# One GNN kernel on one core: the gate, statistics, norm and dense stage ahead of the third pass as a pipeline over pairs of blocks

## The chip, the cores and the metric

One NeuronCore of a Trainium2 chip. Its engines are TensorE (PE; its weight loads stand apart as PEld), VectorE (DVE), ScalarE (ACT), GpSimd (POOL) and SyncE (SP, which here only issues DMAs). The metric is the device time of one execution in microseconds; less is better.

## The reference

`x` has 6250 rows of 256 floats, and there are 106250 edges. Four layers follow one another, each as `x = layernorm(x + L(x))`. The stage in question lies between layer 1 and the first edge loop of layer 2:

```python
# end of layer 1: gate is one row of 256, spa one number a node
L1 = x * spa + x + x * gate
x = _layernorm(x + L1)                          # (v - mean) / sqrt(var + 1e-5)
# layer 2, ahead of its sum over the edges
h = jnp.concatenate([x[row], x[col]], axis=-1)
msgs = silu(h @ W1.T + b1) @ W2.T + b2
```

The product with `W1.T` is made once a node and not once an edge: `x @ A + b1` and `x @ B` are two tables of 256 columns. The edge loop takes a row of the first by a product with a one-hot matrix, and a row of the second (`q_table`) by a gather from DRAM.

## The kernel before, in words

The rows of `x` stand in SBUF as 50 blocks of 128 rows (`x_sb`, NBE = 50), in the tile `big`; two blocks are a pair, and there are 25 (PAIRS). Every engine has its own program; they meet only at semaphores, and each engine's wait holds whatever follows it in that program. The stage between the layers runs as these steps, one after the other:

- **Gate and statistics** (VectorE, L1887): for each pair, (gate + 2 + spa) times x in place (L1891), then mean and variance of each row (L1768, L1772), copied aside (L1774). Each step waits for the one ahead of it (`link`).
- **Norm**: one square root and one reciprocal for all blocks (`normalizers`, L1785 to L1792), then 50 times `normalize` in place (L1798).
- **Store**: once all 50 blocks are done, SyncE writes all of `x_sb` to `x2_table` in DRAM in one DMA (L399) and waits for it. From here on `x_sb` isn't read again before the third pass is over; its place is taken by `p3`.
- **Clear** (VectorE): the accumulator `acc` is set to zero (L1900).
- **Dense**: SyncE loads the blocks of a pair back from `x2_table` to `staged_x` (L406); TensorE turns a block (4 of them a pair, L757); ScalarE copies it to `turned` (L1140); TensorE multiplies by the two halves of W1.T (L931 for q, L933 and the bias L934 for the other), in fp32; ScalarE copies q to `hq` (L1151), which SyncE stores to `q_table` (L411); VectorE splits the other product into three bf16 parts with four instructions (L1908 to L1911) and writes them to `p3`. TensorE turns pair i and multiplies pair i-1 in one turn of its loop.
- **Third pass** (888 tiles of 128 edges): GpSimd gathers rows of `q_table` (L531), and waits ahead of the first for all of its stores; VectorE tells TensorE that it may start by `pass_ready`.

GpSimd has nothing to do in this stage. `x_sb` is 256 floats a block, `p3` is three times 256 bf16 numbers, that is 384 floats a block, in the same tile `big`.

## Time and profile before

| | us |
|---|---|
| median of 3 runs | 7678.52 |
| lowest, highest | 7677.68, 7684.38 |
| the profiled execution, device time | 7685.36 |
| its span | 7683.8 |
| busy in it: PE, DVE, POOL, ACT | 5491.4, 4781.7, 4367.7, 1817.7 |

Times in the rows are microseconds from the start of the span, and the duration of one instruction is in ns where the row says mean. An `x4` is four instructions taken together. What stands in brackets is the idle time of that engine ahead of the instruction and what ended it; SPq is the queue of SyncE. PEclk is TensorE's granted clock: 1.00 is 2.4 GHz and 0.50 is 1.2 GHz. A `MATMUL` on fp32 data shows as two instructions.

### The profile page before, as it was taken

How to read it: one execution, taken by the hardware profiler on the slowest of the kernel's cores; microseconds unless marked ns; L12 is line 12 of the kernel's file. 1: busy time of each engine (PE TensorE's matmuls, PEld its weight loads, DVE VectorE, ACT ScalarE, POOL GpSimd, SP SyncE). 2: the span in 40 equal slices, each digit the busy share in tenths (PEclk: the TensorE clock that was granted, in tenths of full speed). 3: DMA queues.
4: the chain of work that ended last, by engine and by line, in shares of the span. 5: the costliest groups of instructions: out<-in, count | busy, mean ns of one | idle time of the engine just before them, and what ended most of it. 6: DMA issues, size and time to landing. Idle time of an engine off the chain costs nothing.

```text
span 7683.8 us, 131635 instructions
## 1 busy us (share of the span) xinstructions
PE 5491.4 (71%) x23656; PEld 3592.6 (47%) x23657; DVE 4781.7 (62%) x13613; ACT 1817.7 (24%) x3090; POOL 4367.7 (57%) x4491
## 2 busy tenths in 40 slices
PE   5566667799999979399999979815655555656650
PEld 4333334467777658265555545413333333333330
DVE  8878787567777769667777755564344433444435
ACT  4100000168888720033333323300000000000000
POOL 0377777557777730027777730005777777777760
PEclk7577778799999985599999989966555555555555
DMA  3244444443333313233333350011111123111122
GB/s 91 47 124 124 123 125 130 105 133 103 103 103 103 104 26 120 70 100 105 104 105 105 105 92 0 6 45 56 52 52 52 52 51 52 52 52 52 52 51 65
DMA packets 317649, 612.93 MB, mean 80 GB/s; under 512 B 90563, under 2 KB 177804, under 8 KB 317130
## 3 DMA queue, kind: packets, MB, share of 16 engines
q0 software_dynamic: 185408, 469.86, 23.1%
q1 hardware_dynamic: 132106, 141.78, 6.1%
q14 instruction: 113, 0.93, 0.0%
q8 instruction: 22, 0.36, 0.0%
HBM read 573.87 MB, written 43.84 MB: 80 GB/s over the span
## 4 chain that ended last, share of the span: by engine, by line
PE 47%; issue 19%; DVE 15%; DMA 12%; DVEq 3%; POOL 3%; ACT 0%; SPq 0%; POOLq 0%; ACTq 0%
PE bank L751 14%; PE bank L835 8%; PE bank L824 6%; DMA ring<-q_table,stage_i 5%; PE bank L784 5%; DMA ring<-fwd_table,stage_i 3%; DMA ring<-bwd_table,stage_i 2%; POOL ring L531 2%; DVE oh L1652 2%; PE bank L727 2%; DVE ring L1946 1%; DVE big L1503 1%; PE bank L719 1%; PE bank L985 1%; PE bank L986 1%
## 5 line engine op out<-in xcount | busy, mean ns | idle before, releaser
L1641 DVE TENSOR_TENSOR acc<-bank,acc 128x256 f32 (+1 forms) x3552 | 1272.2, 358 | 1681.5 <-PE bank L751 1324.8
L751 PE MATMUL bank<-ring,oh 128*128 128x128 f32 x3552 | 1336.1, 485 | 916.1 <-issue 619.3
L751 PEld LDWEIGHTS bank<-ring,oh 128*128 128x128 f32 x3552 | 884.7, 312 | 1367.6 <-issue 1026.9
L531 POOL DMA_INDIRECT ring<-fwd_table,stage_i x888 | 846.5, 953 | 1006.1 <-issue 937.3
L531 POOL DMA_INDIRECT ring<-q_table,stage_i x888 | 843.3, 950 | 900.9 <-issue 795.1
L531 POOL DMA_INDIRECT ring<-h_table,stage_i x888 | 860.2, 969 | 374.8 <-PE bank L824 192.9
L531 POOL DMA_INDIRECT ring<-bwd_table,stage_i x888 | 842.2, 948 | 274.9 <-issue 156.3
L1166 ACT ACTIVATE ring<-big 128x889 f16<-128x889 f16 x840 | 874.1, 1041 | 199.6 <-PE bank L835 164.5
L835 PE MATMUL bank<-ring,big 128*128 128x445 f16 (+1 forms) x3360 | 773.8, 352 | 0.0
L1652 DVE TENSOR_SCALAR oh<-iota,d_loc,d_norm 128x128 f32<-128x128 f32 x1776 | 658.6, 374 | 70.3 <-DVE big L1725 20.3
L557 POOL DMA_INDIRECT big<-x_and_degree,stage_i x536 | 552.2, 1030 | 201.9 <-issue 118.6
L824 PE MATMUL bank<-ring,oh 128*128 128x256 f32 x1776 | 574.1, 407 | 53.5 <-DVE oh L1652 47.4
L784 PE MATMUL bank<-big,oh 128*128 128x256 f32 x1072 | 443.6, 548 | 228.4 <-DVE oh L1652 224.3
L835 PEld LDWEIGHTS bank<-ring,big 128*128 128x128 f16 x3360 | 483.6, 144 | 161.6 <-issue 0.3
L970 PE MATMUL bank<-ring,oh 128*128 128x257 f32 x1776 | 533.6, 415 | 8.1 <-ACT ring L1251 3.9
L954 PE MATMUL bank<-big,oht 128*128 x2664 | 412.6, 282 | 91.1 <-DVE ring L1946 43.8
L1937 DVE TENSOR_TENSOR acc<-bank,acc 128x257 f32 x888 | 377.1, 425 | 148.6 <-DVE acc L1937 50.7
L784 PEld LDWEIGHTS bank<-big,oh 128*128 128x128 f32 x1072 | 234.2, 255 | 408.7 <-DVE oh L1652 290.2
L557 POOL DMA_INDIRECT ring<-x_and_degree,stage_i x352 | 359.6, 1022 | 107.1 <-issue 69.8
L1946 DVE TENSOR_TENSOR ring<-bank,ring 128x512 f32<-128x512 f32 x444 | 305.0, 687 | 157.8 <-DMA ring<-q_table,stage_i 142.0
L1251 ACT ACTIVATE ring<-ring 128x512 f32<-128x512 f32 x444 | 280.1, 631 | 481.3 <-DVE ring L1946 481.1
L824 PEld LDWEIGHTS bank<-ring,oh 128*128 128x128 f32 x1776 | 298.8, 194 | 198.4 <-issue 76.4
(385 smaller groups left out, 7023.3 us busy)
## 6 DMA issues: line engine op xcount, KB each, us to landing
big<-places_in_block SPq DMA_DIRECT2D x111, 256.0 KB, 3.5
acc<-places_in_block SPq DMA_DIRECT2D x74, 384.0 KB, 3.5
ring<-h_table,stage_i POOLq DMA_INDIRECT x888
ring<-q_table,stage_i POOLq DMA_INDIRECT x888
ring<-fwd_table,stage_i POOLq DMA_INDIRECT x888
ring<-bwd_table,stage_i POOLq DMA_INDIRECT x888
big<-x_and_degree,stage_i POOLq DMA_INDIRECT x536, 3.0
h_table<-hq SPq DMA_DIRECT2D x50, 128.0 KB, 1.7
```

Source lines behind the costliest of these rows:

```text
L531: pool.indirect_dma_start(out=gbuf[:, u % RING, 0:width], out_offset=None, in_=table, in_offset=bass.IndirectOffsetOnAxis(ap=stage_i[:, v, ...
L557: pool.indirect_dma_start(out=first_bufs[v][:, r, 0:D + 1], out_offset=None, in_=xd_dram, in_offset=bass.IndirectOffsetOnAxis(ap=stage_i[: ...
L751: pe.matmul(bank[u % 4][:, 0:width], oh[:, u % 4, :], gbuf[:, u % RING, 0:width], start=True, stop=True).then_inc(S["mm"], 1)
L784: pe.matmul(bank[u % 4][:, 0:D], oh[:, u % 4, :], first_bufs[v][:, r, 0:D], start=True, stop=True).then_inc(S["mm"], 1)
L824: pe.matmul(bank[u % 4][:, 0:D], oh[:, u % 4, :], gbuf[:, r, 0:D], start=True, stop=True).then_inc(S["mm"], 1)
L835: mm = pe.matmul(bank[4 + 2 * k + h][:, 0:hi - lo], low_k[2 * w + k][:, :, r:r + 1].rearrange("p n a -> p (n a)"), high_k[(u + 2 * RING) % ...
L954: mm = pe.matmul(bank[2 + u // 2][:, u % 2 * D:(u % 2 + 1) * D], oht[:, h % 2, u * P:(u + 1) * P], p3[:, s, ds(b, 1), :].rearrange("p a f ...
L970: pe.matmul(bank[4 + u][:, 0:D + 1], oh[:, t % 12, :], msg[:, t % RING, :], start=True, stop=True).then_inc(S["l2_c"], 1)
L1166: act.activation(high_k[u % 3], iota_h, ACT.Sign, bias=high_bias[:, ds(j, 1)]).then_inc(S["sort_high"], 1)
L1641: dve.tensor_tensor(to, bank[u % 4][:, 0:width], to, ALU.add).then_inc(S["accd"], 1)
L1652: o = dve.tensor_scalar(oh[:, u % 4, :], iota[:, :], loc[:, t], weight[:, t], ALU.is_equal, ALU.mult)
L1946: dve.tensor_tensor(msg[:, both, 0:D], bank[2 + t // 2 % 2][:, :].rearrange("p (r f) -> p r f", r=2), gbuf[:, both, 0:D], ALU.add).then_in ...
```

## The change

The stage is written as a pipeline over the 25 pairs. Every engine runs turns t = 0, 1, 2, ...; in turn t it does its step for pair t - lag, where the lag is the step's own. The turns short of the largest lag and those at the end are written out, the others are a loop of two turns (`staggered`). The lags:

| step | engine | pair in turn t |
|---|---|---|
| gate; statistics; their sum to mean and variance | DVE | t; t-1; t-2 |
| square root | ACT | t-3 |
| reciprocal, norm into `x2_buf` | DVE | t-4 |
| store of `x2_buf` to `x2_table` | SP | in the order x2(0), x2(1), q(0), x2(2), q(1), ... |
| turning (4) | PE | t-5 |
| copy to `turned` | ACT | t-6 |
| the two products | PE | t-7 |
| first part of p3, copy to `hq` | ACT | t-8 |
| first rest | DVE | t-9 |
| second part of p3 | ACT | t-10 |
| third part of p3 | DVE | t-11 |

Blocks are taken from the last to the first (`countdown`), and `p3` is laid out by block, so that its parts can be written to `big` while lower blocks of `x_sb` are still to be read. The normed pair goes to one of two buffers `x2_buf`, in the upper half of `ring`; TensorE turns it from there, so that nothing is loaded back. SyncE stores it pair by pair. GpSimd sets `acc` to zero, from `spa_in` on. The counter `p_diff` starts at 2, `x2_out` at 0 and `d_h` at NBE + 2.

The change, cut to its core:

```diff
+def staggered(engine, turns, lag, step):
+    for t in range(lag):
+        step(t, t % 2)
+    twice = (turns - lag) // 2
+    with engine.Fori(0, twice) as i:
+        for k in range(2):
+            step(i * 2 + lag + k, (lag + k) % 2)
+    for t in range(lag + 2 * twice, turns + lag):
+        step(t, t % 2)
...
-        p3 = big[:, :].bitcast(BF16).rearrange("p (s b f) -> p s b f", s=3, f=D)
+        p3 = big[:, :].bitcast(BF16).rearrange("p (b s f) -> p s b f", s=3, f=D)
...
+        x2_buf, rest_p = ([ring[:, LATER + a + 512 * k:LATER + a + 512 * (k + 1)] for k in range(2)] for a in (0, 1024))
...
-            sp.wait_ge(S["x2_done"], NBE)
-            sp.dma_start(x2_dram.rearrange("(b p) f -> p b f", p=P), x_sb).then_inc(S["p_loaded"], 16)
-            sp.wait_ge(S["p_loaded"], 16)
...
+            def store_x2(i, k, n):
+                sp.wait_ge(S["x2_done"], i + 1)
+                apart(sp, S["sp_waited"])
+                if not (isinstance(i, int) and i == 0):
+                    sp.wait_ge(S["x2_out"], i * 16)
+                apart(sp, S["sp_waited"])
+                sp.dma_start(x2_dram[ds(n * P, 2 * P), :].rearrange("(q p) f -> p q f", p=P),
+                             x2_buf[k].rearrange("p (q f) -> p q f", q=2)).then_inc(S["x2_out"], 16)
+            def store_q(i, n):
                 for q in range(2):
-                    sp.wait_ge(S["d_t"], i * 2 + q + 1 + 2 * NBE)
-                    sp.dma_start(staged_x[:, q, :], dense_rows(x2_dram, i * 2 + q)).then_inc(pair["p_in"][q], 16)
-            def store_q(i):
-                for q in range(2):
-                    sp.wait_ge(S["d_h"], i * 2 + q + 3 + NBE)
-                    sp.dma_start(dense_rows(q_dram, i * 2 + q), hq[:, q, :]).then_inc(pair["tab_out"][q], 16)
-            load_pair(0)
-            load_pair(1)
-            with sp.Fori(2, PAIRS) as i:
-                load_pair(i)
-                store_q(i - 2)
-            store_q(PAIRS - 2)
-            store_q(PAIRS - 1)
+                    sp.wait_ge(S["d_h"], i * 2 + 4 + NBE)
+                    apart(sp, S["sp_waited"])
+                    sp.dma_start(dense_rows(q_dram, n + q), hq[:, q, :]).then_inc(pair["tab_out"][q], 16)
+            store_x2(0, 0, 2 * (PAIRS - 1))
+            with sp.Fori(0, PAIRS // 2) as i:
+                for k in range(2):
+                    n = countdown(sp, i * 2 + 1 + k, PAIRS)
+                    store_x2(i * 2 + 1 + k, 1 - k, n)
+                    store_q(i * 2 + k, n + 2)
+            store_q(PAIRS - 1, 0)
+            sp.wait_ge(S["x2_out"], 16 * PAIRS)
...
+            pool.wait_ge(S["spa_in"], 1)
+            pool.memset(acc_flat, 0.0).then_inc(S["acc_clear"], 1)
...
+            def d4_turn(t, par):
+                i, k2 = t - 5, (par + 1) % 2
+                if in_range(i, PAIRS):
+                    pe.wait_ge(S["x2_done"], i + 1)
+                    pe.wait_ge(S["d_at"], i * 2 + 2 * NBE)
                     for q in range(2):
+                        for k in range(2):
+                            mm = pe.transpose(bank[4 + k2][:, k * D + q * P:k * D + (q + 1) * P],
+                                              x2_buf[k2][:, q * D + k * P:q * D + (k + 1) * P], ident[:, :])
+                    mm.then_inc(S["d_t"], 2)
+                i, k2 = t - 7, (par + 1) % 2
+                if in_range(i, PAIRS):
+                    pe.wait_ge(S["d_at"], i * 2 + 4 + 2 * NBE)
+                    pe.wait_ge(S["p_diff"], i + 1)
+                    pe.wait_ge(S["d_h"], i * 2 + NBE)
+                    for q in range(2):
+                        for k in range(2):
+                            pe.matmul(bank[6 + k2][:, q * D:(q + 1) * D], turned[:, k2, k * D + q * P:k * D + (q + 1) * P], w_ab[:, k, 0:D], start=(k == 0), stop=False)
+                        pe.matmul(bank[6 + k2][:, q * D:(q + 1) * D], ones_b[:, :], bias_parts[:, D:2 * D], start=False, stop=True)
+                    for q in range(2):
+                        for k in range(2):
+                            mm = pe.matmul(bank[2 + k2][:, q * D:(q + 1) * D], turned[:, k2, k * D + q * P:k * D + (q + 1) * P], w_ab[:, k, D:2 * D], start=(k == 0), stop=(k == 1))
+                    mm.then_inc(S["d_m"], 2)
+            staggered(pe, PAIRS, 7, d4_turn)
...
+            def d4_functions(t, par):
+                last = countdown(act, t, PAIRS)
+                i, k2 = t - 3, (par + 1) % 2
+                if in_range(i, PAIRS):
+                    act.wait_ge(S["x2_agg"], i + 1)
+                    act.activation(std_k[k2].rearrange("p q a -> p (q a)"), mv_k[k2][:, :, 1:2].rearrange("p q a -> p (q a)"), ACT.Sqrt,
+                                   bias=cols[:, 10:11]).then_inc(S["x2_std"], 1)
+                i, k2 = t - 6, par
+                if in_range(i, PAIRS):
+                    act.wait_ge(S["d_t"], i * 2 + 4 + 2 * NBE)
+                    act.wait_ge(S["d_m"], i * 2 + 2 * NBE)
+                    act.activation(turned[:, k2, :], bank[4 + k2][:, :], ACT.Copy).then_inc(S["d_at"], 2)
+                i, k2 = t - 8, par
+                if in_range(i, PAIRS):
+                    n = last + 16
+                    act.wait_ge(S["d_m"], i * 2 + 4 + 2 * NBE)
+                    act.activation(p3[:, 0, ds(n, 2), :], bank[6 + k2][:, :].rearrange("p (q f) -> p q f", q=2), ACT.Copy).then_inc(S["p_high"], 1)
+                    if not (isinstance(i, int) and i == 0):
+                        for q in range(2):
+                            act.wait_ge(pair["tab_out"][q], BASE["tab_out"] + i * 16)
+                    act.activation(hq[:, :, :], bank[2 + k2][:, :].rearrange("p (q f) -> p q f", q=2), ACT.Copy).then_inc(S["d_h"], 2)
+                i, k2 = t - 10, par
+                if in_range(i, PAIRS):
+                    n = last + 20
+                    act.wait_ge(S["p_diff"], i + 1 + 2)
+                    act.activation(p3[:, 1, ds(n, 2), :], rest_p[k2].rearrange("p (q f) -> p q f", q=2), ACT.Copy).then_inc(S["p_mid"], 1)
+            act.activation(cols[:, 12:13], half_less[:, 0:1], ACT.Sqrt)
+            staggered(act, PAIRS, 10, d4_functions)
...
+            def d4_turn(t, par):
+                last = countdown(dve, t, PAIRS)
+                both_of = lambda s, n: p3[:, s, ds(n, 2), :]
+                by_block = lambda a: a.rearrange("p (q f) -> p q f", q=2)
+                i = t - 4
+                if in_range(i, PAIRS):
+                    dve.wait_ge(S["x2_std"], i + 1)
+                    inverse = std_k[par].rearrange("p q a -> p (q a)")
+                    dve.reciprocal(inverse, inverse).then_inc(S["x2_inv"], 1)
+                i = t - 11
+                if in_range(i, PAIRS):
+                    dve.wait_ge(S["p_mid"], i + 1)
+                    dve.tensor_tensor(both_of(2, last + 22), by_block(rest_p[1 - par]), both_of(1, last + 22), ALU.subtract).then_inc(S["p_split"], 1)
+                i = t - 4
+                if in_range(i, PAIRS):
+                    dve.wait_ge(S["x2_inv"], i + 1)
+                    dve.wait_ge(S["d_t"], i * 2 + 2 * NBE)
+                    if not (isinstance(i, int) and i < 2):
+                        dve.wait_ge(S["x2_out"], i * 16 - 16)
+                    for q in range(2):
+                        n = last + 8 + q
+                        o = dve.tensor_scalar(x2_buf[par][:, q * D:(q + 1) * D], x_of(n), mv_k[par][:, q, 0:1], std_k[par][:, q, :], ALU.subtract, ALU.mult)
+                    o.then_inc(S["x2_done"], 1)
+                i = t - 9
+                if in_range(i, PAIRS):
+                    dve.wait_ge(S["p_high"], i + 1)
+                    if not (isinstance(i, int) and i < 2):
+                        dve.wait_ge(S["p_split"], i - 1)
+                    dve.tensor_tensor(by_block(rest_p[1 - par]), by_block(bank[7 - par][:, :]), both_of(0, last + 18), ALU.subtract).then_inc(S["p_diff"], 1)
+                i = t
+                if in_range(i, PAIRS):
+                    for q in range(2):
+                        n = last + q
+                        o = dve.scalar_tensor_tensor(x_of(n), gate_bc[:, :], sm["spa"][:, ds(n, 1)], x_of(n), ALU.add, ALU.mult)
+                    o.then_inc(S["x2_mul"], 1)
+                i = t - 2
+                if in_range(i, PAIRS):
+                    dve.wait_ge(S["x2_stat"], i + 1)
+                    if not (isinstance(i, int) and i < 2):
+                        dve.wait_ge(S["x2_done"], i - 1)
+                    apart(dve, S["waited"])
+                    for q in range(2):
+                        o = dve.bn_aggr(mv_k[par][:, q, :], stats_k[par][:, q, :])
+                    o.then_inc(S["x2_agg"], 1)
+                i = t - 1
+                if in_range(i, PAIRS):
+                    dve.wait_ge(S["x2_mul"], i + 1)
+                    if not (isinstance(i, int) and i < 2):
+                        dve.wait_ge(S["x2_agg"], i - 1)
+                    for q in range(2):
+                        n = last + 2 + q
+                        o = dve.bn_stats(stats_k[(par + 1) % 2][:, q, :], x_of(n))
+                    o.then_inc(S["x2_stat"], 1)
+            staggered(dve, PAIRS, 11, d4_turn)
+            dve.wait_ge(S["p_split"], PAIRS)
+            dve.wait_ge(S["acc_clear"], 2)
+            dve.wait_ge(S["x2_out"], 16 * PAIRS)
```

## Rows read from the trace of the kernel before

**Rows 1.** Instructions in order of time: the marks between the steps of the stage.

```profile
3126.15 0.88 DVE L1891 SCALAR_TENSOR_TENSOR big<-gate_bc,spa,big 128x256 f32 x2 [0.46 <-DVE gate_bc L1883]
...
3228.07 0.40 SPq L399 DMA_DIRECT2D x_table<-big  x1
3248.40 6.86 SPq L406 DMA_DIRECT2D staged_x<-x_table  x6
3251.12 10.77 DVE L1900 MEMSET acc<- 128x12850 f32 x1 [23.07 <-issue]
```

**Rows 2.** The chain that ended last, in order of time, at the end of the stage.

```profile
3383.16 1.70 DMA q_table<-hq
```

**Rows 3.** The dense step as one stretch: its length, then the columns of the first line.

```profile
core 0: us, PE busy (x) PEld busy (x) DVE busy (x) ACT busy (x) POOL busy (x), PEclk, DMA share, GB/s
3262.00:3385.00 123.00, 116.19 (x520) 81.69 (x520) 78.46 (x201) 31.09 (x94) 0.00 (x0) 1.00 0.30 99
```

**Rows 4.** Instructions in order of time: one pair of the dense step.

```profile
3264.16 0.73 PEld L931 LDWEIGHTS bank<-wbuf,turned 128*128 128x128 f32 x4 [2.51 <-DVE big L1911]
3266.68 0.38 ACT L1151 ACTIVATE hq<-bank 128x256 f32<-128x256 f32 x1
3267.23 2.50 SPq L411 DMA_DIRECT2D q_table<-hq  x2
3268.43 0.98 PE L757 MATMUL bank<-ident,staged_x 128*128 128x128 f32 x4
3268.53 0.38 ACT L1140 ACTIVATE turned<-bank 128x256 f32<-128x256 f32 x1 [1.48 <-PE bank L934]
3269.15 0.73 PEld L931 LDWEIGHTS bank<-wbuf,turned 128*128 128x128 f32 x4
3270.27 0.98 SPq L406 DMA_DIRECT2D staged_x<-x_table  x2
```

**Rows 5.** Groups of instructions by line: busy us, mean ns of one, idle before.

```profile
L1798 DVE TENSOR_SCALAR big<-big,mean,rstd x50 | 20.6, 412 | 4.7 <-DVE rstd L1785 0.4
L1768 DVE BATCH_NORM_STATS2 stats<-big 128x6 f32 x50 | 18.8, 418 | 3.8 <-DVE big L1891 3.8
L1946 DVE TENSOR_TENSOR ring<-bank,ring 128x512 f32<-128x512 f32 x444 | 305.0, 687 | 157.8 <-DMA ring<-q_table,stage_i 142.0
L1246 ACT ACTIVATE oht<-bank 128x512 bf16<-128x512 f32 x79 | 47.2, 597 | 80.5 <-PE bank L962 80.5
```

**Rows 6.** The issues of line L411: ns min/median/max, first and last start.

```profile
L411 SPq DMA_DIRECT2D q_table<-hq x50: 332/356/362, 3259.4 to 3383.2; - x50
```

**Rows 7.** DMA issues: KB each, median us from issue to landing.

```profile
x_table<-big SPq DMA_DIRECT2D x1, 6400.0 KB, 20.3
q_table<-hq SPq DMA_DIRECT2D x50, 128.0 KB, 1.7
```

**Rows 8.** Two pauses of TensorE, in the brackets, in order of time.

```profile
3386.05 0.45 PE L962 MATMUL bank<-ident,oh 128*128 128x128 f32 x1 [3.33 <-issue]
...
4517.86 0.46 PE L970 MATMUL bank<-ring,oh 128*128 128x257 f32 x1 [3.92 <-ACT ring L1251]
```

**Rows 9.** Stretches around changes of the granted clock (columns as in Rows 3).

```profile
3259.00:3260.00 1.00, 1.00 (x6) 0.90 (x5) 1.00 (x1) 0.22 (x1) 0.00 (x0) 0.97 0.00 0
3386.00:3388.00 2.00, 1.09 (x4) 0.72 (x4) 0.73 (x4) 0.60 (x1) 1.70 (x2) 0.50 0.14 31
3392.00:3393.00 1.00, 0.52 (x5) 0.39 (x5) 0.27 (x1) 0.98 (x2) 0.70 (x2) 0.91 0.26 82
4516.00:4518.00 2.00, 0.14 (x1) 0.17 (x2) 1.19 (x3) 0.73 (x2) 0.00 (x0) 1.00 0.00 0
```

**Rows 10.** TensorE's first products of the stage, in order of time.

```profile
3254.32 1.40 PEld L931 LDWEIGHTS bank<-wbuf,turned 128*128 128x128 f32 x4
3258.39 1.04 PEld L931 LDWEIGHTS bank<-wbuf,turned 128*128 128x128 f32 x4 [0.22 <-issue]
```

**Rows 11.** Who SyncE's queue waited for in this stage: us in total, times, longest.

```profile
SPq L411 <- ACT hq L1151: 65.0, 50, 3.9
```

More of the change, by code:

```diff
@@ L42, in runs, with countdown, in_range @@
     return g >= lag if first else g < lag if last else True
+def staggered(engine, turns, lag, step):
[7 more added lines that the diff above has]
+        step(t, t % 2)
+def countdown(engine, t, pairs):
+    return (pairs - 1 - t) * 2 if isinstance(t, int) else engine.snap(t * -2 + (pairs - 1) * 2, min_val=0, max_val=2 * (pairs - 1))
+def in_range(t, turns):
+    return not isinstance(t, int) or 0 <= t < turns
 class Chain:
@@ L1324, in _ @@
             dve.sem_inc(S["slot_prod"], 3)
-            for n in ("d_res", "p_split", "g_ag2", "g_xn", "f_res", "f_out"):
+            for n in ("d_res", "p_diff", "g_ag2", "g_xn", "f_res", "f_out"):
                 dve.sem_inc(S[n], 2)
@@ L1432, in place_blocks @@
                 link(dve.tensor_copy(blk[:, 512:TC], bank[first + 1][:, 0:TC - 512]))
+            dve.memset(cols[:, 10:11], 1e-5)
             link(dve.memset(cols[:, 8:9], 1e-12))
@@ L1885, in _ @@
             dve.wait_ge(S["spa_out"], 1)
-            with dve.Fori(0, PAIRS) as i:
-                chain.enter(i, 4)
-                for q in range(2):
-                    n = i * 2 + q
-                    o = dve.scalar_tensor_tensor(x_of(n), gate_bc[:, :], sm["spa"][:, ds(n, 1)], x_of(n), ALU.add, ALU.mult)
-                link(o)
-                pair_statistics(i)
-            chain.leave(PAIRS)
-            normalizers()
-            with dve.Fori(0, NBE) as b:
-                normalize(x_of(b), b).then_inc(S["x2_done"], 1)
@@ L1912, in _ @@
-            chain.leave(PAIRS)
-            dve.wait_ge(S["p_split"], NBE + 2)
+            def d4_turn(t, par):
[51 more added lines that the diff above has]
+                    o.then_inc(S["x2_stat"], 1)
```

45 lines of the change are left out of this document (7 added, 38 removed).

## The prediction

> **What bounds the kernel now.** I read the page first (span and engines), then the instructions in order of time from the gate to the first gather of the third pass, then stretches, groups and waits of that part. Nothing outside it is touched. The stage runs from 3126.15, the first gate [rows 1], to 3384.86, when the last store of q lands [rows 2]: 258.7 us of 7685.36. The reader is to see three parts that follow one another. Gate, statistics and norm take VectorE alone 101.9 us (3126.15 to 3228.07). The store of all x2 and its wait take 20.3 more, during which nothing computes (3228.07 to 3248.40), and the clearing of the accumulator another 10.8 until 3261.9, over which only three groups of products are made [rows 1]. From 3262 on TensorE is the bound: 116.2 of 123 us busy at a granted clock of 1.00, that is 2.4 GHz [rows 3], one pair from 3264.16 to 3269.15, 4.99 us [rows 4]. VectorE has 78.5 us of work in these 123 and ScalarE 31.1 [rows 3].
>
> **The change, part by part.**
>
> Work per pair after it. VectorE: gate 0.88 [rows 1], statistics 2 x 0.418, norm 2 x 0.412, two subtractions of 512 columns at 0.687 each (the row of a subtraction or sum of that size with one operand in PSUM) [rows 5], some 0.4 for the means and the reciprocal: 4.3 us, and about 5 with the gaps between them. TensorE: the same ten products, 4.4 us from their first weights to ScalarE's start (3264.16 to 3268.53), and four turnings of 0.98 together [rows 4]: 5.3. ScalarE: four copies at 0.597 [rows 5] and a root. SyncE: three issues in place of four. So by work alone a turn is about 5.3 us, and by that the change would gain about 100 us (the first rival). The reload of x2 goes, and so do the 10.8 us of clearing: GpSimd has no other work until the q stores land, so it lies beside them; if it held VectorE up for all its length, that is at most the 10.8 us that VectorE's own clearing took [rows 1]. I take 0. The other layout of p3 and the order from the last block down leave every instruction's size as it is: 0.
>
> What is on the path is a circle of waits that the change makes itself. SyncE's order is x2(m+1), q(m), x2(m+2), q(m+1). A store of q waits for ScalarE's copy of q, and in SyncE's program the next store of x2 stands behind it. VectorE's norm of pair i waits until x2(i-2) has landed (it has two buffers), so it also waits for q(i-4). The lags don't help, because the product that makes q(i-4) itself waits for VectorE: the products of pair j wait for `p_diff` of j+1, which starts at 2, so for the first rest of pair j-2, and VectorE's program has that one right behind the norm of j+3. Followed round: norm of i; first rest of i-5; products of i-3; the two copies of i-3; q(i-3); x2(i-1); its landing; norm of i+1. One round is one pair, and none of its steps lies beside another. Its length:
>
> - norm 0.82 and first rest 0.69 [rows 5]: 1.5
> - products: 4.4 at full clock [rows 4]
> - ScalarE, first part and then q, 2 x 0.597 [rows 5]: 1.2
> - SyncE: 0.17 from the end of a copy (3267.06) to the issue of its store [rows 4]; 0.62 from one issue to the next (0.98 less the 0.36 of an issue [rows 6]); then 0.62 to 0.90 to the store of x2, as 0.90 is what lies between the second q issue (3269.37) and the next load (3270.27) [rows 4]. I take 0.75: 1.5 in all
> - landing of 256 KB: 128 KB took 1.7, and 6400 KB 20.3 [rows 7], so 1.7 + 128 x 18.6 / 6272 = 2.1
> - three hand-overs between engines and the address arithmetic behind each wait, 0.1 each: 0.3. No row shows these waits alone; ends 0 and 1
>
> Sum 11.0 us. TensorE works 4.4 + 1.0 of it and then waits 5.6. That brings in the clock. In the trace TensorE paused for 3.33 us at the end of the stage [rows 8] and came back at 0.50, 1.2 GHz, where it stayed until about 3392.1 [rows 9], 6.1 us later. But after a pause of 3.92 us [rows 8] at 4517.86 the clock was still 1.00 [rows 9]. A pause of 5.6 is longer than both, so I take it that the clock falls in every round. At 1.2 GHz one block's products took 4.07 (3254.32 to 3258.39) [rows 10] against 2.2 (half of the pair's), so a pair takes 8.1 if the clock never rises. It rises during them: 4.7 us after the first products (3254.32 to 3259.0) [rows 9, 10] and 6.1 in the other case. With 4.7 slow the pair takes 4.7 + (8.1 - 4.7) / 2 = 6.4, with 6.1 it takes 7.1. I take 6.4, since here nothing interrupts the burst, and get a round of 13.0; the ends are 11.0 and 14.8.
>
> The Trainium skill, page "TensorE: Matmul & The Clock Gate", section "HAM oscillation — how this bites in real kernels", tells of a kernel whose products come in bursts with a wait for data between them, and whose clock fell anew in each wait. By that rule the round of 11.0 doesn't occur; by the row with the pause of 3.92 us it could.
>
> Sum. Start: pair 0 is normed after four short turns, 4 x 0.88 + 3 x 0.84 + 0.4 + 1.0 and gaps, 7.8 us; pair 2 after two more turns of 3.2, at 14.2; then four turnings and the products of pair 0 at low clock, to 22.0; its copies 23.3; SyncE and landing 3.6, so the norm of pair 4 starts at 26.9. The products of pair 1 need no first rest and follow at once, so the norm of pair 5 starts at 32.2. From there 19 rounds to the norm of pair 24: 19 x 13.0 = 247. End: norm and first rest 1.6, products 6.4, turnings 1.0, three pairs of products without a pause 3 x 4.3, copies 1.2, last store 0.17 + 0.62 + 1.7: 25.6. Together 304.8 us in place of 258.7, **46 us more**. Of what went away, 101.9 of gate and norm now lie beside the rounds, 20.3 + 10.8 are gone; late instead is the store of x2 behind the store of q. The profiled execution would take 7731; it lies 6.9 above the median of the runs, so **7725** there.
>
> **The rivals.**
>
> 1. *The engines run free* (faster): if SyncE's order does not hold the norm back, a turn is bound by TensorE's 5.3 us, 25 x 5.3 = 133, with 8 ahead and 4 behind and a slow start of 4, about 149; if by VectorE's 5 to 5.5 with 11 turns of fill and drain, about 165. 157 gives 102 less: 7577. For it: SyncE waited 65.0 us in all for ScalarE's q in this stage before and delayed nobody [rows 11]. Against it: there the loads behind were two pairs ahead; here the norm needs what is behind, within the same round. It holds if the store of x2 can be two pairs earlier than the waits say. A sentence of the Trainium skill points this way: "DMA: Bandwidth & Descriptors", section "Issuing engines are not separate DMA queues", has it that spreading DMAs over engines saves only the time to initiate them. By it SyncE's order would cost 1.5 us a turn, which is hidden; it doesn't speak of a DMA that stands behind another's wait.
> 2. *The circle holds, the clock stays* (no change): 32.2 + 19 x 11.0 + 23.6 = 264.8, 6 more: 7685. For it the pause of 3.92 us, against it that of 3.33 [rows 8, 9].
> 3. *The circle holds and the clock never rises*: 32.2 + 19 x 14.8 + 27.3 = 340.7, 82 more: 7761. For it that the burst of 6 to 8 us is hardly longer than the 4.7 to 6.1 after which it rose [rows 9, 10].
>
> The turning point between slower and faster is a round of about 10.7 us.
>
> **Chances and range.** The forecast (a round of 12 to 14.2, 7705 to 7748) 0.60; clock stays 0.14; clock never rises 0.11; engines run free 0.12; something else 0.03. 0.2% or 15 us is what a measurement can tell. Faster by more: the free engines and a little of the rest, 0.14. Within: most of the second rival, 0.12. Slower: 0.74. The range takes in the second rival and the third, 7680 to 7765, and leaves out the first, whose place is 100 us off.
>
> **What would show it.** A stage of some 305 us between first gate and first gather; a gate instruction every 13 us from turn 9 on where it is now every 3; VectorE's longest waits ahead of the norm, ended by the DMA to x2_table; SyncE waiting for ScalarE's q; TensorE's clock falling and rising every round with pauses of 5 to 6 us. With free engines the norm would come every 5.3 us and the store of x2 would be issued right after it. A pause without a fall of the clock gives rival 2. If the norm waits for ScalarE or TensorE and not for a DMA, the circle is another one than mine.

## The result, and the profile after

The kernel after the change takes 7766.15 us (median of 5 runs, 7735.88 to 7774.06), beside 7681.53 us of the kernel before on the same chip (5 runs, 7677.68 to 7685.06): ratio 1.0103, 95% interval 1.0089 to 1.0117. It is slower by 85 us, where 46 were forecast. The range, 7680 to 7765, stood against 7678.52 for the kernel before, so it ended 86.5 above that kernel; the 84.6 measured are just inside it, beyond the 7705 to 7748 of the forecast itself, and next to the place of the third rival (82 more). The profiled execution is the one of 7766.15, its span 7764.3.

First the marks of the stage, as in [rows 1]: instructions in order of time, of the kernel after. Columns: start, us, engine, line, operation.

```profile
3130.52 1.67 DVE L1997 SCALAR_TENSOR_TENSOR big<-gate_bc,spa,big 128x256 f32<-128x256 f32 x4 [0.17 <-DVE gate_bc L1956]
...
3158.28 0.74 DVE L1984 TENSOR_SCALAR ring<-big,pair_small 128x256 f32<-128x256 f32 x2 [8.21 <-DMA x_table<-ring]
...
3165.97 0.73 DVE L1984 TENSOR_SCALAR ring<-big,pair_small 128x256 f32<-128x256 f32 x2 [5.30 <-DMA x_table<-ring]
...
3451.09 0.73 DVE L1984 TENSOR_SCALAR ring<-big,pair_small 128x256 f32<-128x256 f32 x2 [11.41 <-DMA x_table<-ring]
...
3469.93 4.33 SPq L440 DMA_DIRECT2D q_table<-hq  x3
```

The L1984 lines are the norms of pairs 4, 5 and 24. The last store of q is issued at 3473.9 (3469.93 + 4.33 less an issue of 0.33) and lands 1.7 us later, at 3475.6. So the stage is 345.1 us where it was 258.7 [rows 1, 2], 86.4 more, which accounts for the 84.6 between the kernels. Its three parts: 35.45 us to the norm of pair 5, 285.12 for the 19 rounds from there to the norm of pair 24 (15.01 each), and 24.5 for the end.

Second, one round of the circle, in order of time, of the kernel after.

```profile
3300.48 0.38 SPq L433 DMA_DIRECT2D x_table<-ring  x1
3302.77 0.74 DVE L1984 TENSOR_SCALAR ring<-big,pair_small 128x256 f32 x2 [11.20 <-DMA x_table<-ring]
3303.42 0.69 DVE L1992 TENSOR_TENSOR ring<-bank,big 128x512 f32<-128x512 f32 x1
...
3304.34 2.07 PE L968 MATMUL bank<-wbuf,turned 128*128 128x256 f32 x4 [6.78 <-DVE ring L1992]
...
3312.87 0.60 ACT L1290 ACTIVATE turned<-bank 128x512 f32<-128x512 f32 x1 [7.49 <-PE bank L972]
3313.37 0.59 ACT L1296 ACTIVATE big<-bank 128x512 f32 x1
3313.85 0.60 ACT L1300 ACTIVATE hq<-bank 128x512 f32<-128x512 f32 x1
3314.32 0.64 ACT L1306 ACTIVATE big<-ring 128x512 f32 x1
3314.70 0.93 SPq L440 DMA_DIRECT2D q_table<-hq  x2
3316.40 0.38 SPq L433 DMA_DIRECT2D x_table<-ring  x1
```

Every link of the predicted circle is there, each behind the one before: the store of x2, its landing and the norm 2.29 us later, norm and first rest (L1992) 1.34, hand-over 0.23, the products until ScalarE's first copy 8.53, ScalarE 1.58 to the end of the copy to `hq` (3314.45), 0.25 to its store, and 1.70 to the next store of x2. That is 15.92 us; rounds of this kind alternate with shorter ones. The brackets name the releasers: VectorE sat 11.20 us until the DMA to x2_table had landed, TensorE 6.78 until the first rest, ScalarE 7.49 until the products.

Third, the same as sums: who waited for whom between 3180 and 3440 (us in total, times, longest).

```profile
DVE ring L1984 <- DMA x_table<-ring: 210.3, 18, 12.4
PEld bank L968 <- issue: 129.4, 35, 7.1
ACT turned L1290 <- PE bank L972: 117.9, 17, 7.5
PE bank L968 <- DVE ring L1992: 101.1, 15, 6.9
```

SyncE's own waits in the whole stage (L27 lies in the helper `apart`, which is called right behind the wait):

```profile
SPq L27 <- ACT hq L1300: 275.1, 25, 13.5
```

Fourth, stretches (columns as in [rows 3]): the body of the stage, and single microseconds of three bursts of products, which start at 3304.34, 3320.16 and 3412.29.

```profile
3180.00:3430.00 250.00, 140.58 (x363) 91.13 (x364) 58.46 (x181) 38.47 (x81) 0.00 (x0) 0.63 0.10 34
...
3313.00:3314.00 1.00, 0.53 (x3) 0.23 (x2) 0.00 (x0) 1.00 (x3) 0.00 (x0) 0.85 0.00 0
...
3320.00:3321.00 1.00, 0.84 (x2) 0.76 (x3) 1.00 (x6) 0.00 (x0) 0.00 (x0) 0.50 0.00 0
3326.00:3327.00 1.00, 1.00 (x4) 0.82 (x3) 0.00 (x0) 0.00 (x0) 0.00 (x0) 0.53 0.00 0
3327.00:3328.00 1.00, 1.00 (x7) 0.85 (x7) 0.00 (x0) 0.06 (x1) 0.00 (x0) 1.00 0.00 0
...
3414.00:3415.00 1.00, 1.00 (x3) 0.52 (x3) 0.00 (x0) 0.00 (x0) 0.00 (x0) 0.50 0.00 0
3415.00:3416.00 1.00, 1.00 (x4) 0.66 (x3) 0.00 (x0) 0.00 (x0) 0.00 (x0) 0.65 0.00 0
3416.00:3417.00 1.00, 1.00 (x6) 0.66 (x5) 0.00 (x0) 0.00 (x0) 0.00 (x0) 1.00 0.00 0
```

TensorE is busy for 140.58 of 250 us and its mean granted clock is 0.63, where it was 116.19 of 123 at 1.00 [rows 3]. In the first burst the clock rises only at 3313.3, 9.0 us after the start and behind the products (ScalarE began to copy at 3312.87); in the second it rises 6.8 us after the start, in the third after 3.4. Over the 19 rounds the products take 8.5 and 7.4 to 7.8 us in turn, and 6.2 to 6.6 in the last few.

Last, something that the prediction had put at nothing. The first norm instructions of the stage and the clearing of `acc` by GpSimd, in order of time, of the kernel after:

```profile
3129.89 10.81 POOL L632 MEMSET acc<- 128x12850 f32 x1 [360.16 <-DVEq L1954]
...
3136.10 5.06 DVE L1984 TENSOR_SCALAR ring<-big,pair_small 128x256 f32<-128x256 f32 x2
...
3142.84 0.73 DVE L1984 TENSOR_SCALAR ring<-big,pair_small 128x256 f32<-128x256 f32 x2
```

The two instructions of pair 0 took 5.06 us, those of pair 1 0.73, and they ended 0.46 us behind the clearing (3136.10 + 5.06 = 3141.16 against 3129.89 + 10.81 = 3140.70), which is about one instruction of this kind: the first of the two was held until the clearing ended.

### The profile page after: what moved, and what is told of

It reads as the page before. It is cut to its first block, busy times and chain, and to the rows that moved or that the text cites. A ratio compares the mean times of both kernels' runs of the same rounds, so it can differ in the third digit from the quotient of the medians.

```text
span 7764.3 us, 130770 instructions
## 1 busy us (share of the span) xinstructions
PE 5559.9 (72%) x23656; PEld 3638.3 (47%) x23657; DVE 4718.5 (61%) x13460; ACT 1844.3 (24%) x3115; POOL 4373.5 (56%) x4492
## 4 chain that ended last, share of the span: by engine, by line
PE 24%; issue 13%; DMA 13%; DVE 5%; POOL 2%; DVEq 1%; SPq 0%; POOLq 0%; ACT 0%; ACTq 0%
PE bank L783 14%; DMA ring<-q_table,stage_i 6%; DMA ring<-fwd_table,stage_i 3%; DMA ring<-bwd_table,stage_i 2%; POOL ring L561 2%; DVE ring L2056 2%; PE bank L1024 1%; PE bank L1025 1%; PE bank L968 1%; PE bank L972 1%; PE bank L1009 1%; DVE oh L1723 1%; PE bank L1029 1%; PE bank L1032 1%; PE bank L993 1%
## 5 line engine op out<-in xcount | busy, mean ns | idle before, releaser
L783 PEld LDWEIGHTS bank<-ring,oh 128*128 128x128 f32 x3552 | 884.6, 311 | 1360.1 <-issue 977.9
L993 PEld LDWEIGHTS bank<-big,oht 128*128 128x128 bf16 x2664 | 255.6, 96 | 292.6 <-issue 209.3
```

What stands on the lines that cost most here:

```text
L783: pe.matmul(bank[u % 4][:, 0:width], oh[:, u % 4, :], gbuf[:, u % RING, 0:width], start=True, stop=True).then_inc(S["mm"], 1)
L993: mm = pe.matmul(bank[2 + u // 2][:, u % 2 * D:(u % 2 + 1) * D], oht[:, h % 2, u * P:(u + 1) * P], p3[:, s, ds(b, 1), :].rearrange("p a f ...
```

## The experiments

### The circle opened at SyncE: x2 stored two pairs ahead

Only the order of SyncE's stores changes; every wait keeps its value. In the kernel after, the store of x2 of pair m stands behind the q of pair m-2; here it stands behind that of pair m-4, and the first four wait for nothing of the circle.

```diff
-            store_x2(0, 0, 2 * (PAIRS - 1))
-            with sp.Fori(0, PAIRS // 2) as i:
-                for k in range(2):
-                    n = countdown(sp, i * 2 + 1 + k, PAIRS)
-                    store_x2(i * 2 + 1 + k, 1 - k, n)
-                    store_q(i * 2 + k, n + 2)
-            store_q(PAIRS - 1, 0)
+            for i in range(3):
+                store_x2(i, i % 2, 2 * (PAIRS - 1 - i))
+            with sp.Fori(0, (PAIRS - 3) // 2) as i:
+                for k in range(2):
+                    n = countdown(sp, i * 2 + 3 + k, PAIRS)
+                    store_x2(i * 2 + 3 + k, 1 - k, n)
+                    store_q(i * 2 + k, n + 6)
+            for m in range(PAIRS - 3, PAIRS):
+                store_q(m, 2 * (PAIRS - 1 - m))
```

> The changed kernel with one edit: SyncE issues the stores of x2 for pairs 0 to 2 first and then x2(m+3), q(m), so no store of x2 stands behind a store of q that isn't ready. Theory A (the circle norm, first rest, products, copies, store of q, store of x2, landing, norm sets the round of about 15.3 us that the changed kernel's profile shows): the circle is cut, the norm no longer waits for a landing, and a round falls to TensorE's 5.3 us at a clock of 1.00 (it then pauses under 1 us); the stage takes about 150 to 165 us in place of 345, and the kernel about 7580. Rival B (the lags themselves are too short, so that VectorE and TensorE wait for each other whatever SyncE does): the round stays over 10 us and the kernel over 7680. Rival C (the store to DRAM is what is slow, not its place): the norm still waits for the landing, round of 8 or more.

Measured: 7564.11 us (4 runs, 7562.13 to 7565.93), ratio to the kernel before 0.9848, interval 0.9831 to 0.9864. From its profile a stretch, a wait, and two stores of x2 that are one pair apart:

```profile
3150.00:3250.00 100.00, 100.00 (x470) 73.38 (x470) 67.67 (x207) 46.28 (x101) 0.00 (x0) 1.00 0.32 109
```

```profile
DVE ring L1986 <- DMA x_table<-ring: 2.1, 1, 2.1
```

```profile
3234.75 0.38 SPq L433 DMA_DIRECT2D x_table<-ring  x1
...
3239.19 0.38 SPq L433 DMA_DIRECT2D x_table<-ring  x1
```

TensorE is busy for all of the 100 us at full clock, VectorE waits 2.1 us for a DMA in that stretch, and a pair takes 4.70 us on average (the stores come 4.44 and 4.98 us apart in turn). The stage is 137.3 us, from 3129.20 to 3266.54. So the same instructions on every engine, with the same waits and one other order of issue, move the kernel by 202 us. The place of the store in SyncE's program is the cause, and this version beats both kernels.

### The same with one pair ahead

The store of x2 of pair m stands behind the q of pair m-3; the rest is as above.

```diff
+            for i in range(2):
+                store_x2(i, i % 2, 2 * (PAIRS - 1 - i))
+            with sp.Fori(0, (PAIRS - 3) // 2) as i:
+                for k in range(2):
+                    n = countdown(sp, i * 2 + 2 + k, PAIRS)
+                    store_x2(i * 2 + 2 + k, k, n)
+                    store_q(i * 2 + k, n + 4)
+            store_x2(PAIRS - 1, (PAIRS - 1) % 2, 0)
...
```

> The changed kernel with the store of x2 one pair earlier on SyncE than in the change: x2(m+2), q(m). Theory A says how long a round is: the same circle now goes round in two pairs, so at full clock its 11.7 us give 5.9 a pair, against 4.70 in x2_two_ahead, where TensorE was the bound; 19 pairs of 1.2 us make some 20 to 25 us, so the kernel at 7585 to 7595 if the clock stays at 1.00, and up to 7620 if it falls at times. If only the fact counts that a store of x2 stands behind one of q, as it still does here for the pair before, the kernel stays over 7700.

Measured: 7591.10 us (2 runs, 7587.71 to 7594.49), ratio 0.9879 (0.9859 to 0.9899). The waits of VectorE between 3180 and 3270:

```profile
DVE ring L1987 <- DMA x_table<-ring: 26.7, 13, 3.0
```

The granted clock over these 90 us is 0.91. The circle still closes, but with the other order one trip round it leads from the norm of pair i to that of i+2, so it serves two pairs: 12.0 us for two at a clock of 1.00 (from norm to norm, 3195.57 to 3207.60), and 13.6 from there on (3207.60 to 3221.22), where the clock falls once in every two pairs; the free engines need 9.4. A stage of 171.3 us lies between 345.1 and 137.3.

By the same count a trip serves three pairs when x2 is stored two pairs ahead. An estimate from the 12.0 us is then 4.0 a pair, less than the 4.70 for which TensorE is busy. So in that version the circle isn't gone: it is short enough to hold nobody up.

### The stores of q issued by ScalarE

SyncE stores x2 alone; ScalarE issues the store of q behind its own copy to `hq`.

```diff
-                    store_q(i * 2 + k, n + 2)
-            store_q(PAIRS - 1, 0)
...
                     act.activation(hq[:, :, :], ...).then_inc(S["d_h"], 2)
+                    act.wait_ge(S["d_h"], i * 2 + 4 + NBE)
+                    for q in range(2):
+                        apart(act, S["act_waited"])
+                        act.dma_start(dense_rows(q_dram, n + q), hq[:, q, :]).then_inc(pair["tab_out"][q], 16)
```

> The changed kernel with the stores of q issued by ScalarE, right after its copy, in place of SyncE; SyncE has only the stores of x2 left. Theory A: as with the other order on SyncE, a round of 5.3 to 5.6 us and the kernel at about 7580, as ScalarE has some 2.9 us of work a turn and the two issues and the wait for its own copy add about 1.5. Rival F (a queue of its own only saves the time to issue, 1.5 us a round): round of 13.5 to 14, kernel about 7725.

Measured: 7577.81 us (2 runs, 7576.57 to 7579.05), ratio 0.9865 (0.9845 to 0.9884). All stores of x2 in one row, in order of time:

```profile
3142.01 117.90 SPq L433 DMA_DIRECT2D x_table<-ring  x25
```

25 stores in 117.9 us are one in 4.9 us, and between 3150 and 3250 VectorE never waited for a DMA. It is 14 us behind the version with x2 two pairs ahead: ScalarE now issues too (between 3150 and 3250 its copy L1307 waited 14 times for issue, 19.1 us). This takes the link between the two stores out of SyncE's program altogether. The Trainium skill, page "DMA: Bandwidth & Descriptors", section "Issuing engines are not separate DMA queues", has it that spreading DMAs over engines saves only the time to initiate them. Here the spreading was worth 188 us (7766.15 against 7577.81, each beside about 7681 of before), since what it took away was a wait in the program of the issuing engine; the page doesn't speak of that case, and the measurement decides it.

### VectorE takes the first rest ahead of the norm

The first rest of pair t-9 moves ahead of the norm of pair t-4 within a turn of VectorE, so that the products of t-7 no longer stand behind the norm of t-4.

```diff
+                i = t - 9
+                if in_range(i, PAIRS):
+                    dve.wait_ge(S["p_high"], i + 1)
+                    ...
+                    dve.tensor_tensor(by_block(rest_p[1 - par]), by_block(bank[7 - par][:, :]), both_of(0, last + 18), ALU.subtract).then_inc(S["p_diff"], 1)
                 i = t - 4
                 if in_range(i, PAIRS):
                     dve.wait_ge(S["x2_inv"], i + 1)
...
-                i = t - 9
-                ...
```

> The changed kernel with SyncE's order kept and one edit in VectorE's turn: the first rest of pair t-9 ahead of the norm of pair t-4 and not behind it. Theory A: the circle then goes round only once in two pairs (norm of i-1, rest of i-5 comes ahead of norm of i, products of i-3, copies, store of q, store of x2, norm of i+1), so the round about halves: 7.7 to 9 us with the remaining waits, the stage about 195 to 245, the kernel about 7620 to 7660. Rival E (SyncE waiting for q is the whole cause, and VectorE's order is of no account): round and time as in the changed kernel, 7735 to 7775.

Measured: 7638.43 us (2 runs, 7638.34 and 7638.52), ratio 0.9944 (0.9924 to 0.9964). The waits between 3180 and 3300, and the stretch itself:

```profile
DVE ring L1991 <- DMA x_table<-ring: 63.1, 14, 5.7
```

```profile
3180.00:3300.00 120.00, 91.39 (x313) 59.80 (x313) 51.30 (x154) 32.91 (x70) 0.00 (x0) 0.81 0.19 64
```

A round (norm to norm) takes 7.8 us and 8.0 to 9.6 in turn, 8.4 on average, and the stage 214.1. VectorE still waits for the DMA, 4.5 us each time in place of 11.7 (210.3 / 18). So the link from norm to first rest in VectorE's program is part of the circle too; what remains is a shorter circle, not free engines.

### What the clock takes: TensorE kept busy in its pause

The circle stays, and TensorE gets products whose result nobody reads (128x512, fp32, from `ident` and `wbuf` into a bank that is free then) ahead of its wait for the first rest; they are work added, and nothing is left out. Five of them first, seven in a later kernel.

```diff
                 i, k2 = t - 7, (par + 1) % 2
                 if in_range(i, PAIRS):
+                    for f in range(5):
+                        pe.matmul(bank[0][:, :], ident[:, :], wbuf[:, 0:512], start=True, stop=True)
```

> The changed kernel with SyncE's order kept. TensorE makes five more fp32 products of 128x512 a turn, into a bank that nobody reads, ahead of its wait for the first rest; they only fill its pause. At full clock they take 5 x 0.85 = 4.3 us of a pause of 6.7. Theory A1 (the circle stays, and TensorE's low clock makes the products 8 us in place of 4.4): the clock stays near 1.00 in the stage, products take 4.4, a round falls from 15.3 to about 11.5 and the stage from 345 to about 275, the kernel to about 7700, and its runs spread less. Rival D (the products are slow for another reason, for instance their order or the waits between them): they stay at 8 us, the round grows by what the extra work sticks out of the pause, and the kernel is at 7770 or above.

Measured: 7760.36 us (4 runs, 7759.62 to 7761.28), ratio 1.0102 (1.0085 to 1.0119). This missed, and the rows say why. TensorE in order of time, and the microsecond in which the clock fell:

```profile
3288.25 4.46 PE L964 MATMUL bank<-wbuf,ident 128*128 128x512 f32 x10
3295.19 1.13 PE L970 MATMUL bank<-wbuf,turned 128*128 128x256 f32 x4 [2.49 <-DVE ring L1994]
```

```profile
3296.00:3297.00 1.00, 1.00 (x4) 0.53 (x3) 1.00 (x4) 0.23 (x1) 0.00 (x0) 0.62 0.00 0
```

The five filled 4.46 of some 7 us. A pause of 2.49 us stayed, and the clock fell just behind it, within the products. Of 18 such pauses between 3197 and 3436 (2.3 to 2.7 us) the clock fell at or just behind 12 and stayed up at 6. The rounds took 13.7 us on average in place of 15.01, and the ends of the stage grew. So this run couldn't price the clock, and the filler was lengthened to seven.

> As fill_pause, with seven products of 128x512 in place of five: at full clock 7 x 0.89 = 6.2 us of a pause of 6.7 (in fill_pause the trace showed a pause of 2.5 us left, and the clock fell 3.7 us after it began). Theory A1 (the circle stays, the pause puts the clock down and so makes the products 8 us): with a pause of 0.5 us the clock stays at 1.00, the products take 4.4, a round 11.8 and the stage about 280 us in place of 345; the kernel at 7700 to 7715. Rival D (the products are slow for another reason than the clock): round of 15 or more, kernel at 7765 or above.

Measured: 7733.74 us (4 runs, 7731.35 to 7734.88), ratio 1.0064 (1.0047 to 1.0081). The stretch, VectorE's wait in it, and TensorE in order of time:

```profile
3180.00:3400.00 220.00, 204.86 (x673) 112.61 (x673) 60.45 (x186) 44.74 (x93) 0.00 (x0) 1.00 0.13 45
```

```profile
DVE ring L1986 <- DMA x_table<-ring: 151.3, 18, 9.7
```

```profile
3300.31 6.17 PE L964 MATMUL bank<-wbuf,ident 128*128 128x512 f32 x14
3307.26 1.13 PE L970 MATMUL bank<-wbuf,turned 128*128 128x256 f32 x4 [0.78 <-DVE ring L1994]
```

The clock is now 1.00 over 220 us, TensorE is busy for 204.86 of them, and the kernel is still 49 us slower than before. By the parts of the stage some 27 of these are the filler's own, at its two ends (below); the other 22 are the circle's, without any low clock in its rounds. The round is 11.8 us where the second rival's sum said 11.0, and 15.01 without filler. So the clock was worth 3.2 us a round, 61 us over 19 rounds; only 32 of them show in the time, and it missed the 7700 to 7715 expected. The filler of 6.2 us a turn also stands ahead of products at the two ends of the stage, where there was no pause to fill, and start and end together are 86.8 us (46.2 and 40.6 of a stage of 311.1) in place of 60.0. A busy TensorE at full clock isn't a bound: with 93% busy this stage was 311.1 us, and with less work on TensorE it was 137.3.

The kernel after was run once more beside fill_all and x2_one_ahead.

> The changed kernel as it is, beside the others on this chip. Its five runs so far gave 7736 to 7774. Theory A1: no round's wait changes, only in how many rounds the clock comes up early; expected 7735 to 7775 again, and more spread than the kernels whose clock stays up.

Measured: 7769.97 us (4 runs, 7742.11 to 7776.52), ratio 1.0104 (1.0082 to 1.0126), as the first time. Its runs spread over 34 us, and over 38 the first time, where those of the two kernels with filler spread over 1.7 and 3.5. In its profile the 19 rounds take 288.6 us, in the first one 285.1: the last three rounds were 13.2 to 13.7 us long there, here one was.

### GpSimd's clearing and VectorE's norm

The kernel before with one part of the change alone: GpSimd clears `acc`, VectorE no longer does.

```diff
-            link(dve.memset(acc_flat, 0.0))
...
+            pool.wait_ge(S["spa_in"], 1)
+            pool.memset(acc_flat, 0.0).then_inc(S["acc_clear"], 1)
...
+            dve.wait_ge(S["acc_clear"], 2)
```

> The kernel before with one part of the change alone: GpSimd clears acc from spa_in on, VectorE doesn't. Expected: VectorE's 10.8 us go, but TensorE worked beside them until 3260.9; it gains the 2.5 us that its products of pair 1 waited for VectorE, and perhaps a few more where its clock rises no earlier: 2 to 8 us, so 7673 to 7679, hardly measurable. If the clearing was worth its full length, 7670.

Measured: 7687.22 us (10 runs, 7682.94 to 7690.50), ratio 1.0005 (0.9995 to 1.0014). No gain, where 2 to 8 us were expected and though VectorE has 10.8 us less to do. In order of time, of this kernel:

```profile
3125.07 10.81 POOL L602 MEMSET acc<- 128x12850 f32 x1 [359.18 <-DVEq L1883]
...
3126.01 0.88 DVE L1893 SCALAR_TENSOR_TENSOR big<-gate_bc,spa,big 128x256 f32 x2 [0.48 <-DVE gate_bc L1885]
3127.04 0.75 DVE L1770 BATCH_NORM_STATS2 stats<-big 128x6 f32 x2
...
3128.33 7.58 DVE L1776 TENSOR_SCALAR mv<-mv_one 128x4 f32 x1
...
3141.79 0.17 DVE L1776 TENSOR_SCALAR mv<-mv_one 128x4 f32 x1
...
3255.68 6.79 SPq L406 DMA_DIRECT2D staged_x<-x_table  x6
```

An instruction of 4 columns took 7.58 us and ended with the clearing (3125.07 + 10.81 = 3135.88); elsewhere it takes 0.17. Everything behind it is late by as much: the first load of x2 comes 129.7 us after the first gate, where it was 122.3 [rows 1]. The gate instruction and the statistics, which ran beside the clearing, took their usual 0.88 and 0.75 for two. So the clearing doesn't lie beside VectorE's work: it stops one kind of it, shown here for a tensor_scalar that reads and writes SBUF. The tensor_scalar that writes `gate_bc` from PSUM began 0.03 us behind the clearing in the kernel after (3129.92) and took its usual 0.42.

To tell "they exclude each other, one instruction at a time" from "GpSimd keeps hold of something for all its clearing", the clearing was cut into ten.

```diff
-            pool.memset(acc_flat, 0.0).then_inc(S["acc_clear"], 1)
+            for k in range(10):
+                pool.memset(acc_flat[:, 1285 * k:1285 * (k + 1)], 0.0).then_inc(S["acc_clear"], 1)
...
+            dve.wait_ge(S["acc_clear"], 11)
```

> The kernel before with the clearing of acc by GpSimd, as in clear_on_pool, but in ten pieces of 128x1285. In clear_on_pool a VectorE tensor_scalar of 128x4 took 7.58 us where the same instruction takes 0.17 otherwise, and ended as the clearing did. Theory (they exclude each other, instruction by instruction): it takes under 1.3 us here, one piece at most, and the same for those after it while pieces are left; the first load of x2 is issued at about 3250, 1 to 2 us after that of the kernel before (3248.40) where it was 7.3 us late (3255.68), and the time is 3 to 7 us under that of clear_on_pool, 7680 to 7684 us. Rival (GpSimd holds VectorE from the first piece to the last): as in clear_on_pool, 7687 us.

Measured: ratio to the kernel before 0.9997 (0.9984 to 1.0011). This and the next kernel ran on another chip, on which the kernel before took 9282.28 us (17 runs) and this one 9278.26 (12 runs); so only the ratio and the stretches of the stage can be set beside the others, and the interval is too wide for the 3 to 7 us. The trace tells more. In order of time:

```profile
3666.61 11.24 POOL L603 MEMSET acc<- 128x1285 f32 x10 [366.73 <-DVEq L1884]
...
3669.86 0.17 DVE L1777 TENSOR_SCALAR mv<-mv_one 128x4 f32 x1
...
3672.89 0.49 DVE L1777 TENSOR_SCALAR mv<-mv_one 128x4 f32 x1
```

The instruction is held for 0.3 us twice, and not at all in the turn before; the first load of x2 comes 122.9 us after the first gate (3667.54 to 3790.45), 0.7 more than in [rows 1] in place of 7.4. They take turns, instruction by instruction. The same cut in the fast version:

> The kernel with x2 stored two pairs ahead, and in it GpSimd's one clearing of acc (128x12850, 10.81 us) cut into ten clearings of 128x1285; everything else as it was. Theory (a VectorE tensor_scalar on SBUF can't run while a GpSimd memset does, and takes its turn between two of them): the first pair of norm instructions takes under 2 us where it took 5.05, the first store of x2 is issued 3 to 4.3 us earlier after the stage's begin (it was 10.8 us, 3129.20 to 3140.03), the clearing itself ends some tenths later, and the kernel takes about 7560 us beside 7564, a difference that shows in the trace and hardly in the times. Rival (the first norm waits for something else that comes at that moment, such as the table load of ScalarE or a first use of the instruction): the 5.05 us stay. Second rival (GpSimd holds what VectorE needs from its first piece to its last): the 5.05 us stay too, and clear_in_pieces tells these two apart by whether its statistics instruction is still held.

Measured: ratio to the kernel before 0.9867 (0.9845 to 0.9890), 9161.23 us (4 runs) on that other chip, so no difference to the 0.9848 of the version with one clearing can be read from the times. In order of time:

```profile
3685.71 1.90 DVE L1987 TENSOR_SCALAR ring<-big,pair_small 128x256 f32<-128x256 f32 x2
...
3689.29 1.94 DVE L1987 TENSOR_SCALAR ring<-big,pair_small 128x256 f32<-128x256 f32 x2
...
3692.91 0.74 DVE L1987 TENSOR_SCALAR ring<-big,pair_small 128x256 f32<-128x256 f32 x2
```

The first store of x2 is issued 7.7 us after the first gate (3680.12 to 3687.80) where it was 10.8. Of the 3.2 won, 1.2 go back at pair 1, and from first gate to first gather the stage is 137.6 us, against 138.5 of the version with one clearing (3129.20 to 3267.72). The norms of pairs 0 and 1 are still held, by 1.2 us each. Cutting the clearing made the hold short and brought about 1 us.

## Why the prediction was right or wrong

**The sign and the mechanism were right.** The circle of waits was forecast link by link from the code, and each link shows in the round above. Four kernels that each take away or loosen one link (x2 stored one or two pairs ahead, q stored by ScalarE, first rest ahead of the norm) are all faster than the kernel before, and one that leaves the circle and holds the clock up is slower. That the circle is the cause is shown, not argued.

**The size was off: 345.1 us of stage where 304.8 were forecast.** That the time still lies inside the range is owed to the range, which took in the third rival; the round is not among the 12 to 14.2 us that I held likely. By the prediction's own parts:

| part | forecast | measured |
|---|---|---|
| start, to the norm of pair 5 | 32.2 | 35.45 |
| 19 rounds | 247 (13.0 each) | 285.1 (15.01 each) |
| end | 25.6 | 24.5 |

**The round, term by term** (measured: the round shown above; for the products and SyncE the mean of the 19):

| term | forecast | measured |
|---|---|---|
| norm and first rest | 1.5 | 1.34 |
| products | 6.4 | 7.8 (6.2 to 8.5) |
| ScalarE | 1.2 | 1.58 |
| SyncE, copy to store of x2 | 1.5 | 1.82 (0.25 and 1.44 or 1.70) |
| landing and hand-overs | 2.1 + 0.3 | 2.29 + 0.23 |

**Products, +1.4 a round, two thirds of the miss.** The step that failed is "I take 6.4, since here nothing interrupts the burst". I had two delays of the clock's rise, 4.7 and 6.1 us [rows 8 to 10], and chose the shorter on an argument, not on a row. In the bursts it rose 3.4 to 9.0 us after their start (3412.3 to 3415.7, 3197.8 to 3204.0, 3304.3 to 3313.3), mostly later than either row. In eight of the 19 rounds the products ran at the low clock to their end: 8.53 us, which is near the 8.1 of the third rival. In eight more the clock rose after 5.9 to 6.8 us and they took 7.4 to 7.8, longer than both of my cases. The 6.4 that I took held in the last three alone. So 15.01 lies even above the 14.8 that I had for a clock that never rises, because of the next two terms.

**ScalarE, +0.4.** I counted two copies. ScalarE's turn has three on this path: the copy to `turned` of pair t-6 (L1290) waits for the products of pair t-8, as it writes the buffer that they read, and stands ahead of both. The code showed it; I had not written out ScalarE's turn in its order.

**SyncE, +0.3.** The end that I named for the way to the store of x2, 0.62 to 0.90, was too low for one round in two: 1.70 from the first store of q to that of x2 less 0.62 is 1.08. The store of x2 has two waits of its own and address arithmetic.

**The fall of the clock was right.** With pauses of 6.6 to 6.9 us, and one of 7.6, it fell every time. The row with 3.92 us that spoke for the second rival [rows 8, 9] was read too short: the clock was 1.00 when that pause ended, but it fell 0.7 us later, at 4518.6, within the products. The next stretch of the kernel before shows it:

```profile
4518.00:4520.00 2.00, 2.00 (x6) 1.33 (x7) 1.36 (x4) 0.00 (x0) 0.00 (x0) 0.65 0.00 0
```

So that pause was followed by a fall too, as the one of 2.49 us in the kernel with filler was, and the second rival had no row of its own. Its sum, 11.0 a round, was 11.8 with the filler in: the 0.8 are mainly ScalarE's and SyncE's terms above, 0.38 and 0.32.

**The clearing, taken at 0, held the first norm.** I named the bound (up to 10.8) and took the lower end without a reason from a row. The norm of pair 0 was held 4.3 us (5.06 against 0.73). The whole start came out 3.25 us over its sum. How much of that is the clearing's wasn't measured in this kernel; cut into pieces in the version with x2 two pairs ahead it brought about 1 us. The Trainium skill, page "SBUF — State Buffer", section "Who interferes with whom", has it that VectorE and GpSimd share a pair of ports by an exclusive lock that some VectorE instructions take, `tensor_scalar` among them. These traces agree: tensor_scalar was held (5.06 and 7.58 us), while the gate's scalar_tensor_tensor with two operands in SBUF and the statistics were not.

**The first rival was under-rated in what it can bring, not in its chance.** With SyncE's order changed the engines do run free: 4.70 us a pair, less than the 5.3 that I summed from TensorE's rows, and 137.3 us in place of 157. The sum counted too much: the 4.99 us from one pair's first weights to the next one's [rows 4] already held the turnings. It "holds if the store of x2 can be two pairs earlier", and this is just what the version with x2 two pairs ahead does. The kernel given doesn't.

**Left open.** Why the clock rises after 3.4 us in one burst and after 9.0 in another was not settled; the runs show the spread and that bursts in turn differ. What makes the runs of the kernel after differ by 34 to 38 us isn't shown either. The number of rounds in which the clock comes up early is a candidate, as the two profiles differ in it; against it stands the kernel with five products of filler, in which the clock also fell again and again and whose runs spread over 1.7 us.

## What to carry to other kernels

In a pipeline written out by hand, follow every wait round through the programs of all engines, the DMA issuer's too, until it closes or leaves: lags of several turns are worth nothing if one engine's program puts a store that many wait for behind a result that waits for them. A circle's time is the sum of its latencies and no engine is its bound, so look for it where all engines are half idle; and the cure can be a different order of issue (here 202 us), not less work. Where such a circle makes TensorE work in bursts, count its products at the low clock for the whole burst until a row of the same pattern says better.

## What the runs showed of the hardware that was not expected

- TensorE's granted clock fell to 0.50 after a pause of 2.49 us between two busy stretches (five filler products), and stayed at 1.00 over 220 us where the pauses were 0.8 to 0.9 us (seven). With five it fell at or just behind 12 of 18 such pauses. In the kernel before it fell 0.7 us behind the end of a pause of 3.92 us.
- In bursts of 6 to 8.5 us with pauses of 6.6 to 7.6 between them it rose 3.4 to 9.0 us after the start of a burst; where two bursts came alike, the long and the short one alternated (8.53 and 7.4 to 7.8 us of products).
- A GpSimd memset of 128x12850 (10.81 us) held a VectorE tensor_scalar of 128x4 for 7.4 us; cut into ten of 1.17 us, for 0.3 us. Scalar_tensor_tensor, the statistics and a tensor_scalar that reads PSUM ran beside it at their usual length.
- The same kernel took 7681 us on one chip and 9282 us on another. Of two profiled kernels that differ only in the cut of the clearing, the one there (9277.1 us) had a mean granted clock of 0.707 and moved 66 GB/s on average, the one here (7681.4) 0.745 and 80. What makes the difference wasn't looked into.
